# Cross-attention with a mixture of experts on one core: the shared expert four steps later, and a table that is named column by column

## The reference

```python
x = x + xattn(layernorm(x), ctx, ctx, mask, Wq, bq, Wk, bk, Wv, bv, Wo, bo)     # 16 heads of 16
x = x + ffn(layernorm(x), ...)

def ffn(x, ...):                                    # xf: 4096 x 256
    scores = sigmoid(xf @ gate_weight.T)            # 32 experts
    # 4 of 8 groups of experts by their best corrected score, then 6 experts in them
    tw = chosen scores / (their sum + 1e-20) * 2.5
    routed = sum over experts e of combine[:, e] * (silu(xf @ gate_e.T) * (xf @ up_e.T)) @ down_e.T
    shared = (silu(xf @ shared_gate.T) * (xf @ shared_up.T)) @ shared_down.T    # inner width 256
    return routed + shared
```

## Time and profile before

| | us |
|---|---|
| median of 3 runs (lowest to highest) | 807.67 (807.05 to 809.29) |
| the profiled execution's own time | 806.62 |
| its span in the profile | 804.8 |
| TensorE busy | 721.8 (90% of the span) |
| VectorE, ScalarE, GpSimd busy | 523.9, 391.9, 543.9 |

### The profile page before, as it was taken

One profiled execution on the slowest core, in us unless ns is written; L12 is line 12 of the kernel. 1 busy time (PEld: TensorE's weight loads), 2 busy tenths in 40 slices (PEclk: granted clock), 3 DMA queues, 4 the chain that ended last, 5 costly groups with the idle time before them and its releaser, 6 DMA issues.

```text
span 804.8 us, 18561 instructions
## 1 busy us (share of the span) xinstructions
PE 721.8 (90%) x5760; PEld 647.3 (80%) x5760; DVE 523.9 (65%) x1608; ACT 391.9 (49%) x834; POOL 543.9 (68%) x811
## 2 busy tenths in 40 slices
PE   3699999999999999996737999999999999999960
PEld 2478988898888898883426999999999999999950
DVE  4847777777787777773471223577777676667773
ACT  0155544545444554440104666666666666666630
POOL 0202887887888788888800002888889888888885
PEclk9789999999999999998977999999999999999995
DMA  9202444433433332222763556888899998898972
GB/s 292 71 28 60 132 125 133 131 121 109 125 128 125 131 100 73 86 85 81 250 218 95 171 171 183 251 252 270 266 274 271 276 269 264 266 274 265 277 219 72
DMA packets 112930, 140.66 MB, mean 175 GB/s; under 512 B 16625, under 2 KB 99957, under 8 KB 112706
## 3 DMA queue, kind: packets, MB, share of 16 engines
q1 hardware_dynamic: 90584, 85.94, 34.6%
q0 software_dynamic: 18432, 50.36, 20.5%
q10 hardware_dynamic: 3818, 3.19, 1.3%
HBM read 76.36 MB, written 63.06 MB: 173 GB/s over the span
## 4 chain that ended last, share of the span: by engine, by line
PE 48%; POOL 33%; issue 10%; DMA 3%; DVE 3%; ACTq 1%; SPq 0%; POOLq 0%; ACT 0%; DVEq 0%
PE sc_ps L944 25%; POOL rows L488 21%; PE bank L954 12%; POOL firsts L479 7%; PE sc_ps L928 6%; POOL rstd L495 2%; POOL work L518 2%; DMA work<-tabd 1%; DMA wdn<-in_gate_b 1%; PE sc_ps L831 1%; DVE firsts L976 1%; PE bank L844 1%; POOL work L479 1%; PE bank L753 1%; PE bank L670 1%
## 5 line engine op out<-in xcount | busy, mean ns | idle before, releaser
L944 PE MATMUL sc_ps<-work 128*128 128x128 f32 x1792 | 220.0, 276 | 0.0
L518 POOL DMA_INDIRECT work<-yrows,dest x192 | 189.8, 989 | 34.3 <-POOL work L479 25.5
L944 PEld LDWEIGHTS sc_ps<-work 128*128 128x128 f32 x1792 | 210.5, 193 | 0.4 <-ACT work L624 0.3
L488 POOL DMA_INDIRECT rows<-work,dest x192 | 188.1, 979 | 32.4 <-issue 31.8
L479 POOL MEMSET work<- 128x304 f32 x192 | 75.7, 394 | 93.8 <-DMA yrows<-work 92.1
L1365 DVE TENSOR_TENSOR work<-work,sc_ps 128x256 f32<-128x256 f32 x112 | 47.0, 420 | 120.0 <-ACT work L629 118.8
L954 PE MATMUL bank<-wdn,work 128*128 x448 | 115.3, 380 | 0.1
L651 ACT ACTIVATE work<-bank 128x512 f32<-128x512 f32 x112 | 66.9, 597 | 53.1 <-PE bank L954 52.5
L1391 DVE SCALAR_TENSOR_TENSOR work<-work 128x256 f32<-128x256 f32 x160 | 76.9, 480 | 12.9 <-DMA work<-yrows,dest 9.7
L954 PEld LDWEIGHTS bank<-wdn,work 128*128 128x128 f32 x448 | 76.6, 191 | 6.3 <-issue 0.5
L624 ACT ACTIVATE work<-sc_ps 128x512 f32<-128x512 f32 x112 | 66.3, 592 | 31.3 <-PE sc_ps L928 31.3
(11 more groups left out here) (176 smaller groups left out, 1148.5 us busy)
## 6 DMA issues: line engine op xcount, KB each, us to landing
work<-rows SPq DMA_DIRECT2D x224, 128.0 KB
yrows<-work SPq DMA_DIRECT2D x224, 128.0 KB
wgu<-in_egu SPq DMA_DIRECT2D x16, 512.0 KB, 4.1
store<-in_x SPq DMA_DIRECT2D x8, 512.0 KB, 9.8
wdn<-in_edn SPq DMA_DIRECT2D x8, 512.0 KB, 4.0
out<-work SPq DMA_DIRECT2D x32, 128.0 KB
rows<-work,dest POOLq DMA_INDIRECT x192, 2.5
work<-yrows,dest POOLq DMA_INDIRECT x192
```

What stands on the lines that cost most here:

```text
L488: pool.indirect_dma_start(rows[:, :], bass.IndirectOffsetOnAxis(ap=dest[:, t, k:k + 1], axis=0), rowb[:, m, :], None).then_inc(scat[m], 16)
L518: pool.indirect_dma_start(yg[:, g % RG, :], None, yrows[0:n * P, :], bass.IndirectOffsetOnAxis(ap=dest[:, t, k:k + 1], axis=0)).then_inc(l ...
L944: last = mm(ps8[2 + m % 2][:, (2 * w + g) * P:(2 * w + g + 1) * P], wst[w][m % 2][:, k * 2 * I + g * I:k * 2 * I + (g + 1) * I], xeT[:, m ...
```

## The change

- **Lag.** `up`, `half_tanh`, `dn`, `gated`, `add_shared` go from lags 4, 5, 5, 5, 6 to 8, 9, 9, 9, 10 (SHL = 8), and the waits of `qk` with them. The ring of x1 has eight slots, at the place of the last eight experts' down weights, also for tiles 24 to 27. SP loads 24 experts' down weights in the loop; the last two groups of four follow behind the sums that free their slots, before the wait for the table. The first `s_up` of the stage between waits for the last tile's shared expert.
- **GpSimd's order.** The power op stands between the two halves of a tile's scatters.
- **Table.** SP loads two of the four arrays into `pc`, eight entries of each per partition (8 KB in pieces of 32 bytes). `name_blocks` is now eight ops: column c of `oh` is, in 256 places, the entry's value where the place's number (`jrow`, loaded with the constants) is the entry's block. TensorE sums them over partitions and columns by eight matmuls with a column of ones. It stands behind `s_hidden` and `s_base`.
- **Addresses.** Three of the arrays are loaded to all partitions only behind the first twelve tile loads, 512 KB each, into slots of `yg`; the third when two address ops are done. The five ops run in pair steps 1, 2, 6, 7 and 8, the slots from step 9 on.
- **Queues.** Tails: SP 4 and 6, ScalarE 4, 6, 6 and 6. SP's twelve tile loads have no pause, and TensorE waits for down weights only at its first `down`.

The diff, without its context lines and without the lists of names:

```diff
...
-NX = NT - B - TS
+NX = 8
+SHL = 8
...
 def _const_layout():
-                    ("jtile", 2), ("third", 3), ("half_neg", E), ("tri", P), ("ones", P), ("rep", HCOLS),
+                    ("third", 3), ("half_neg", E), ("tri", P), ("ones", P), ("rep", HCOLS),
...
-    put("jtile", p + P * np.arange(2)[None] + 1)
+    c[:, NCONST:] = np.arange(2 * P)[None] + 1
...
-        sched = sb("sched", [P, 2])
+        pc = sb("pc", [P, 2, E * NT // P])
...
-        xn, xnT, qT, o, oT, _, probs, pT, rowb, wq_sb, wo_sb, wg_sb, kbd, vbd, maskb, repb = att
+        xn, xnT, qT, o, oT, spare1, probs, pT, rowb, wq_sb, wo_sb, wg_sb, kbd, vbd, maskb, repb = att
+        jrow = spare1.rearrange("p a d -> p (a d)")[:, 0:2 * P]
-            slot = t % 4 if t < TS else t - TS
-            return x1w[:, slot * D:(slot + 1) * D]
+            return x1w[:, t % NX * D:(t % NX + 1) * D]
-            return x1w[:, (t - TS) * D:(t - TS + 2) * D].rearrange("p (b d) -> p b d", b=2)
+            return x1w[:, t % NX * D:(t % NX + 2) * D].rearrange("p (b d) -> p b d", b=2)
...
+        bcA = yg[:, 0:4, :].rearrange("p a (e t) -> p (a e) t", t=NT)
+        bcB = yg[:, 4:8, :].rearrange("p a (e t) -> p (a e) t", t=NT)
-        bc, at = carve(work, 4 * D, [P, 4, E, NT])
-        told, at = carve(work, at, [P, E, NT])
+        oh, at = carve(work, 12 * 256, [P, E * NT // P, 2 * P])
...
-        TAILS = [0, 4, 16, 20, 24, 28, E]
+        TAILS = [0, 4, 10, 14, 20, 26, E]
...
         def _(sp):
-            sp.dma_start(cst[:, :], const_in[:, :]).then_inc(S_["ld_const"], 16)
+            sp.dma_start(cst[:, :], const_in[:, 0:NCONST]).then_inc(S_["ld_const"], 16)
...
+            sp.dma_start(jrow, const_in[:, NCONST:NCONST + 2 * P]).then_inc(S_["ld_s"], 16)
...
-            sp.dma_start(bc[:, :, :, :].rearrange("p q e t -> p (q e t)"),
-                         tabd.rearrange("(a q) e t -> a (q e t)", a=1).broadcast_to([P, 4 * E * NT])
+            sp.dma_start(pc[:, :, :], tabd[0:2].rearrange("q e t -> q (e t)").rearrange("q (p c) -> p q c", p=P)
+            need(sp, "sbase", TS - 1)
+            ld_down(E - 4)
+            need(sp, "base", SB - 2 - SE, 2)
+            ld_down(E - 8)
-                sp.wait_ge(tails_st[q], 16 * ((5, 12, 16)[q]))
+                sp.wait_ge(tails_st[q], 16 * ((5, 6, 22)[q]))
...
-            for j in range(4):
+            def ld_bc(q, to):
+                sp.dma_start(to.rearrange("p e t -> p (e t)"), tabd[q:q + 1].rearrange("q e t -> q (e t)").broadcast_to([P, E * NT])
+                             ).then_inc(S_["bc_ld"], 16)
+            for j in range(RX):
-            need(sp, "yaddr", 0, 5)
-            for j in range(4, RX):
-                ld_tile(j)
-            for s in range(SE, SB - 1):
-                need(sp, "base", s - SE, 2)
-                ld_down(E - NX + 4 * (s - SE))
+            need(sp, "base", SB - 1 - SE, 2)
+            ld_bc(1, bcA)
+            ld_bc(3, bcB)
+                if n == 3:
+                    need(sp, "yaddr", 1)
+                    ld_bc(2, bcB)
...
             def step(tile):
+                at_tile(tile, 0, inverse_std)
-                at_tile(tile, 0, inverse_std)
...
-                at_tile(tile, 5, half_tanh)
+                at_tile(tile, SHL + 1, half_tanh)
...
             def qk(t, m, s):
-                if 0 <= t - 5 < TS:
-                    need(pe, "hidt", t - 5, 2)
-                if 0 <= t - 6 < TS:
-                    need(pe, "sbase", t - 6)
+                if 0 <= t - 1 - SHL < TS:
+                    need(pe, "hidt", t - 1 - SHL, 2)
+                if 0 <= t - 2 - SHL < TS:
+                    need(pe, "sbase", t - 2 - SHL)
...
-                    pe.wait_ge(S_["ld_s"], 32)
-                need(pe, "score_sub0", t + 4)
+                    pe.wait_ge(S_["ld_s"], 48)
+                need(pe, "score_sub0", t + SHL)
...
-                need(pe, "score_sub0", t + 5)
+                need(pe, "score_sub0", min(t + SHL + 1, NT - 1))
...
             def s_early(t, m, s):
+                    need(pe, "hidt", TS - 1, 2)
+                    need(pe, "sbase", TS - 1)
...
-                at_tile(tile, 4, up)
-                at_tile(tile, 5, dn)
+                at_tile(tile, SHL, up)
+                at_tile(tile, SHL + 1, dn)
...
             def lay_table():
-                need(pe, "sched", 0, 2)
-                for i in range(2):
-                    last = mm(sch_ps[:, i * P:(i + 1) * P], sched[:, i:i + 1], ident, start=True, stop=True)
+                for c in range(E * NT // P):
+                    need(pe, "named", c)
+                    last = mm(sch_ps, const("ones")[:, 0:1], oh[:, c, :], start=c == 0, stop=c == E * NT // P - 1)
...
-            pe.wait_ge(S_["ld_edn"], 16 * (E // 4))
...
             def down(i, m, q):
+                if i == 0:
+                    pe.wait_ge(S_["ld_edn"], 16 * (E // 4))
...
             def residual(t, m, s):
-                if 4 <= t < TS + 4:
-                    need(v, "sbase", t - 4)
+                if NX <= t < TS + NX:
+                    need(v, "sbase", t - NX)
...
-                at_tile(tile, 5, gated(0))
-                at_tile(tile, 6, add_shared)
-                at_tile(tile, 5, gated(1))
+                at_tile(tile, SHL + 1, gated(0))
+                at_tile(tile, SHL + 2, add_shared)
+                at_tile(tile, SHL + 1, gated(1))
...
-            def name_blocks(i):
+            def name_blocks():
-                if i == 1:
-                    need(v, "sched", 0)
-                v.scalar_tensor_tensor(told[:, :, :], bc[:, 0, :, :], const("jtile")[:, i:i + 1], bc[:, 1, :, :],
-                                       ALU.is_equal, ALU.mult, accum_out=sched[:, i:i + 1]).then_inc(S_["sched"], 1)
+                v.wait_ge(S_["ld_s"], 48)
+                for c in range(E * NT // P):
+                    ts(oh[:, c, :], jrow, pc[:, 0, c:c + 1], pc[:, 1, c:c + 1], ALU.is_equal,
+                       ALU.mult).then_inc(S_["named"], 1)
...
             def address_rows(i):
-                    v.wait_ge(S_["sched"], 2)
-                    v.scalar_tensor_tensor(told[:, :, :], place[:, :, :], float(E), bc[:, 1, :, :], ALU.mult,
-                                           ALU.is_ge).then_inc(S_["yaddr"], 1)
+                    v.wait_ge(S_["bc_ld"], 32)
+                    v.scalar_tensor_tensor(bcA, place[:, :, :], float(E), bcA, ALU.mult, ALU.is_ge).then_inc(S_["yaddr"], 1)
-                    tt(told[:, :, :], told[:, :, :], bc[:, 3, :, :], ALU.mult).then_inc(S_["yaddr"], 1)
+                    tt(bcA, bcA, bcB, ALU.mult).then_inc(S_["yaddr"], 1)
-                    tt(told[:, :, :], told[:, :, :], bc[:, 2, :, :], ALU.add).then_inc(S_["yaddr"], 1)
+                    v.wait_ge(S_["bc_ld"], 48)
+                    tt(bcA, bcA, bcB, ALU.add).then_inc(S_["yaddr"], 1)
-                    tt(told[:, :, :], told[:, :, :], place[:, :, :], ALU.add).then_inc(S_["yaddr"], 1)
+                    tt(bcA, bcA, place[:, :, :], ALU.add).then_inc(S_["yaddr"], 1)
-                    v.scalar_tensor_tensor(place[:, :, :], place[:, :, :], 0.0, told[:, :, :], ALU.is_gt,
+                    v.scalar_tensor_tensor(place[:, :, :], place[:, :, :], 0.0, bcA, ALU.is_gt,
...
-                    if s == SE + 1:
-                        name_blocks(h)
-                    if s == SE + 2:
-                        address_rows(h)
+                    name_blocks()
-                if s == SE + 2:
-                    address_rows(2)
-                    address_rows(3)
-                    address_rows(4)
-            address_slots(0, 8)
...
+            ADDRESS = (1, 2, 6, 7, 8)
-                if 8 <= n < NT:
-                    address_slots(n, n + 1)
+                if n in ADDRESS:
+                    address_rows(ADDRESS.index(n))
+                if n in (9, 10):
+                    address_slots(5 * (n - 9), 5 * (n - 8))
+                if 11 <= n < NT:
+                    address_slots(n - 1, n)
+                if n == NT:
+                    address_slots(NT - 1, NT)
...
```

More of the change, by code:

```diff
@@ L66, in constants @@
 def constants():
-    c = np.zeros((P, NCONST), np.float32)
+    c = np.zeros((P, NCONST + 2 * P), np.float32)
     def put(name, a):
@@ L278, in build @@
                      "gate_add score sfc group expert sel wsel rank place dest selcum "
-                     "counts tail_rows cum_ps fresh pos_ps sch tab tab_st tab_ld sched sch_ps table yaddr dest2 "
+                     "counts tail_rows cum_ps fresh pos_ps sch tab tab_st tab_ld bc_ld named sch_ps table yaddr dest2 "
                      "ld_s up_ps th hidt dn_ps sbase sg_ps shg shh sy_ps base wnorm "
```

## The result

The median after is 798.83 us (4 runs, 798.14 to 803.15), beside 808.48 for the kernel before on the same chip (807.05 to 811.35): ratio 0.9883, interval [0.9843, 0.9923]. Run again beside the first group of experiments (`again`), it took 798.21 us against 807.7: 0.9906 [0.9877, 0.9935]. So the change gains 7.6 to 9.7 us. The forecast was 15.9 (792.0 us, range 787.5 to 799.5): right in sign and inside the range, near its slow end; the gain is 0.5 to 0.6 of the forecast's.

The account below looks back on a forecast made before the run. No engine bounds the whole; a chain of waits runs through tile loop, stage between and expert stage. First pair -17.3 and addresses +1.4 give -15.9 on 806.62, 790.7; plus 1.05 to the median, 792 us; range 787.5 to 799.5.

Parts of the forecast that it names:

- Lag: Tile loop: shared expert eight steps behind makes steps 4 to 7 light; last power op at 372.2, 4.6 us earlier.
- GpSimd's order: Tile loop: 21 scatters follow the last power op, ending at 404.0 against 404.19; with the lag, scatters' end stays.
- Table: Stage between: write lands at 390.7, small load takes 3.0 us, table ready at about 401.7, base by 406.7.
- Addresses: Expert stage: five address ops of 1.22 us, mostly hidden in VectorE's idle time; +1.4 us from the op at n = 1.
- wait at the second pair: Expert stage, n = 1: address op waits for two 512 KB broadcasts landing at 421.3; +1.4 us, bounds 0 and 4.7.
- The narrow forecast: Whole kernel: median between 787.5 and 793.5 us, around the forecast of 792; chance 0.45.
- the forecast's own signs of being wrong: Changed profile: variance step above 10.6 us, SP's loads behind rows of zeros after 410, or gathers' spacing leaving 1.57.
- Rival B: Tile loop does not shorten: last power op stays at 376.8, scatters end at 408.6; 4.6 us more, 796.4; chance 0.15.
- Rival D: Tile loop: normalised rows' ring of four waits for scatters landing slower than 6.5 us; about 811 us; chance 0.03.
- SP's queue: Before expert stage: weight wait gone, scatters' landing opens loads; first pair at 410.9 against 428.24, -17.3 us.
- Rival A: Gate before expert stage: scatters' landings stay slow at 6.2 us, gate 3.7 us later, 795.5 us; chance 0.2.
- The third broadcast: Expert stage: issued at SP's n = 3, has 9 us until n = 6, so costs nothing.

Follow-up runs that it names:

- profile on record: The changed kernel itself, unaltered: its first profiled execution, with TensorE's clock low in the set-up; 803.15 us, span 801.0.
- fill_half: `wdn_late` plus four matmul instructions with unread results in each of the four light steps; 797.01 us, ratio 0.9847 to the kernel before.
- tails_bc_2: `tails_bc` run again on another chip, beside `fill_half`; 796.27 us, ratio 0.9837 to the kernel before.
- tails: The changed kernel with six of ScalarE's 22 rows of zeros moved to SP's queue; 814.47 us on a chip where before takes 825.8, ratio 0.9865.
- tails_bc: `tails` with the two address broadcasts behind six tile loads instead of twelve; 813.86 us on a chip where before takes 825.8, ratio 0.9866.
- wdn_late: `tails_bc` with the last two weight loads (1 MB) moved behind the fourth tile load; 794.84 us, ratio 0.9844 to the kernel before.

## Why the prediction was right or wrong

The forecast's stations against `again`, both from the span's start:

| station | forecast | measured | added to the error |
|---|---|---|---|
| last power op | 372.2 | 375.40 | +3.2 |
| first tile load | 407.6 | 413.58 | +2.8 |
| first pair | 410.9 | 415.77 | -1.1 |
| pair to first gate matmul | 1.86 as before (430.10-428.24) | 3.71 | +1.85 |
| wait at the second pair | 1.4 | 0.64 | -0.8 |

Together +6.0; the spans differ by 795.0-788.9 = 6.1 (788.9 is the forecast's 790.7 less the 1.8 around the span).

The time lies in the range because the range was wide, not because the path was foreseen. The narrow forecast (787.5 to 793.5) missed, no rival has the gate or the tanh wait behind ScalarE's issues, and two of the forecast's own signs of being wrong came: SP starts its loads behind rows of zeros at 413.58, after 410, and a variance step lies above 10.6 (12.77 in the profile on record).

1. **Lag: the step that failed first.** "V(5) = 66.29+7.92 = 74.2", then 82.1: measured 8.69 and 9.49 us. The 7.92 was TensorE's work at full clock, and the forecast let the clock stay when the work left; it also had no wait, where TensorE stood 0.56 us for ScalarE in the first light step (8.13 busy). And 1.1 of the 4.2 us is its own sum: two steps of 9.5 behind 82.1 give 101.1, not "about 100". Rival B, "the light steps stall on GpSimd or TensorE's clock", is what happened, with 1.4 us left of 4.6. GpSimd's 9.5 in the third step did not bind either: `fill_half` shows 8.82 there, with GpSimd busy for 7.57 of it. The other end was right: 10.58 up to step 30, 9.47 in step 31.
2. **GpSimd's order.** Right: the last scatter starts 30.8 us behind the last power op (406.23), as forecast, and the time shows no effect. Rival D did not show: the ring of `rowb` cost no step anything (10.58 us each).
3. **Table.** The load was rightly put near the write, and faster than forecast: both were taken at 3.0 us; SP's wait for the write was 1.1, and the issues' medians to landing are 1.5 and 2.0 us. The Trainium skill (DMA: Bandwidth & Descriptors, Specifications) gives 512 bytes as the least piece for line rate; the load's pieces have 32, and at 8 KB in all no such cost shows in its 2.0 us. What failed is "the table at about 401.7": it came at 411.5. The prediction saw the six more rows of zeros on ScalarE's queue, took issues at 0.55 us each and "hidden under the scatters", and never asked who waits behind them on ScalarE; six took 5.74 us there with their addresses. In `tails_bc_2`, with six of them moved, the table is ready 31.4 us after the power op, in `tails` 33.4, in `again` 36.1. A second term was too small: the naming matmuls were to end 0.4 us behind VectorE, and VectorE waited 2.68 us for them. In `again` TensorE had stood idle 4.79 us before them, and they took 5.37 us at a granted clock of 0.63 and then 0.80; in `tails_bc_2` 4.03 us, with a wait of 0.78.
4. **SP's queue.** "What is late next is the scatters' landing" is wrong for the change: it is the zeros of ScalarE's queue, issued until 407.7. Rival A's number (795.5) was nearer than the forecast's, as was B's (796.4), but A's mechanism (the scatters' landing of 6.2 us) was not it; the landing of the last zeros was 4.84. Right was that the wait for weights, 13.19 us, would go whole. The cover that the forecast counted on for VectorE ("sums of weights and first copy, some 4 us behind base, fit before 412.8") was missing: the first copy ended at 419.19. But the last wait of the first gate matmuls is for ScalarE's transposed tiles, 1.02 us, behind waits of 0.29 and 0.78 for the tiles' own landing, and in `tails_bc_2`, where the copy ended at 414.96, pair to gate still takes 3.31 us (at a granted clock of 0.50). So the 1.85 is a term that the sum took over from before: there the tiles were issued 4.1 to 14.7 us ahead of the first pair, and its transposes ran without a wait.
5. **Addresses.** The wait at the second pair was there, 2.8 us on VectorE, and 0.64 in the pair's period (the gate matmuls start at 426.37 and 430.10, 3.73 apart instead of 3.09; the 0.97 in the expectation of `tails_bc` does not come out of the trace): forecast 1.4. The third broadcast cost nothing. The gathers' spacing stayed: (786.53-485.51)/191 = 1.576 us.

The best version measured is `wdn_late` (794.8 us) or `tails_bc_2` (796.3), which their ratios, 0.9844 and 0.9837, don't tell apart, though the profiled spans are 2.7 us apart (791.5 and 794.2) and 2.5 to 3 us were expected; both are some 2 to 5 us below the change (by the medians 1.9 to 4.0, by the ratios to before 3.2 to 5.6).

## What to carry to other kernels

A DMA issue is work of the engine whose queue it is put on: before rows are moved to a queue, look for the next compute instruction of that engine, and who waits for it. If work is taken out of a stretch that TensorE fills, its price at full clock is the most that can come back; look where the idle time would fall, and try a little filler there (here it shortened the loop; that it pays in the median was not shown). And when a chain is shortened, read who issued the transfer that opens the next gate, not only what it is.

## What was not expected of the hardware

- TensorE's granted clock fell to 0.82 and 0.76 in steps in which TensorE had 78 or 79 matmul records instead of 94 or 98; with 86 it stayed at 1.00, so that more work took less time (36.00 us for 38.04).
- The set-up, the same in all kernels, runs in one of two ways: V(3) at 58.5 to 60.1 us or at 63.2 to 64.3. The four late profiles have a granted clock of 0.78 to 0.84 from 20 to 30 us, the ten others 1.00. Here `again` first, then the profile on record:

```profile
20.00:30.00 10.00, 7.45 (x37) 5.37 (x38) 9.82 (x37) 2.12 (x5) 2.94 (x1) 1.00 0.45 157
```

```profile
20.00:30.00 10.00, 9.67 (x37) 7.25 (x36) 7.05 (x27) 1.23 (x4) 2.94 (x1) 0.78 0.52 178
```

- A DMA share near 1.0 (0.99 to 1.08) went with 293 to 391 GB/s.
- The expert stage starts at half clock after TensorE's wait at the gate: the first gate matmuls take 3.75 us for sixteen records in `tails_bc_2` and `wdn_late`, at a granted clock of 0.50, where the earlier trace rows have 1.95 for as many. The kernel before has the same (3.58 us at 0.55), so the change does not alter it. The wait costs 1.6 to 1.8 us more than its length.
- A load of 8 KB in 32-byte pieces to 128 partitions landed in 2.0 us.
